# A bias that TensorE multiplied in is copied by ScalarE, and two convolution parts change place

## What is computed

```python
h = tok(x)                                    # conv, relu, batch norm: (16, 252, 256)
sim = q @ k.T * scale + bias[head, i - j]     # causal, 16 heads of 16
h = h + softmax(sim) @ v @ Wo + bo            # q, k, v from layernorm(h)
h = h + ffn_quantised(layernorm(h))           # 256 -> 768 -> 256
```

## Time and profile before

| | before |
|---|---|
| median of 3 runs | 801.44 us (800.09 to 801.98) |
| the profiled execution, own time | 804.09 us |
| its span, first to last instruction | 802.1 us |
| attention stage / feed-forward stage | to about 497 us / from there on |
| one step in the middle of the attention stage | 26.8 us |
| PE, DVE, ACT busy over the span | 78%, 76%, 57% |

### The profile page before, as it was taken

One profiled execution on the slowest core, in us unless ns is written; L12 is line 12 of the kernel. 1 busy time (PEld: TensorE's weight loads), 2 busy tenths in 40 slices (PEclk: granted clock), 3 DMA queues, 4 the chain that ended last, 5 costly groups with the idle time before them and its releaser, 6 DMA issues. The chain is left out here.

```text
span 802.1 us, 14667 instructions
## 1 busy us (share of the span) xinstructions
PE 625.1 (78%) x5169; PEld 463.1 (58%) x5169; DVE 610.3 (76%) x966; ACT 456.5 (57%) x647; POOL 134.7 (17%) x211
## 2 busy tenths in 40 slices
PE   4588899889988998899889975989999800005998
PEld 3457777767776777677767654335444300004997
DVE  7436787888788878888888787687479998994442
ACT  1436456545654565456545643426389966967772
POOL 4221122122213221322132000000024320000000
PEclk9789999999999999999999875899999955555999
DMA  7324313412441244124412311100134144400433
GB/s 199 114 30 48 40 21 61 62 26 33 59 59 25 34 59 59 23 36 59 61 25 30 55 54 53 39 1 0 44 150 194 44 188 145 138 0 1 145 118 100
DMA packets 39204, 52.82 MB, mean 66 GB/s; under 512 B 5724, under 2 KB 31772, under 8 KB 39164
## 3 DMA queue, kind: packets, MB, share of 16 engines
q1 hardware_dynamic: 38012, 51.49, 28.8%
q10 hardware_dynamic: 1152, 0.79, 0.5%
HBM read 22.74 MB, written 16.81 MB: 49 GB/s over the span
## 5 line engine op out<-in xcount | busy, mean ns | idle before, releaser
L803 DVE TENSOR_REDUCE mx<-ps 126x2 f32<-126x504 f32 (+1 forms) x192 | 125.7, 676 | 33.1 <-PE ps L651 31.8
L794 DVE TENSOR_TENSOR sbr<-ps,biasT 126x504 f32<-126x504 f32 x192 | 120.3, 676 | 27.6 <-PE ps L669 26.1
L879 ACT ACTIVATE pt<-sbr 126x504 f32<-126x504 f32 x192 | 110.9, 618 | 32.3 <-DVE sbr L794 26.1
L669 PE MATMUL ps<-q_st,k_st 66*126 66x252 f16 (+1 forms) x512 | 67.5, 257 | 22.7 <-DVE sbr L794 14.2
L648 PE MATMUL ps<-biasN,antib 126*126 126x504 bf16 x192 | 74.6, 388 | 3.6 <-DMA k_st<-kl 3.6
L651 PE MATMUL ps<-k_st,q_st 65*126 65x252 f16 (+1 forms) x512 | 74.0, 246 | 0.0
L1146 PE MATMUL ps<-x2t,wgT 128*128 128x504 f16 x288 | 67.2, 394 | 8.1 <-ACT gat L1437 4.7
L1423 PE MATMUL ps<-wdT,raws 128*126 128x256 f16 x480 | 67.5, 282 | 4.5 <-DVE raws L1364 4.5
L1122 PE MATMUL ps<-identf,sc 128*128 128x128 f32 x5 | 2.2, 435 | 86.7 <-DVE sc L1354 56.5
L651 PEld LDWEIGHTS ps<-k_st,q_st 65*126 65x126 f16 x512 | 59.6, 137 | 17.3 <-issue 2.5
L669 PEld LDWEIGHTS ps<-q_st,k_st 66*126 66x126 f16 x512 | 50.4, 142 | 32.9 <-DVE sbr L794 19.3
(11 more groups left out here) (189 smaller groups left out, 1405.4 us busy)
## 6 DMA issues: line engine op xcount, KB each, us to landing
up_raw<-raws SPq DMA_DIRECT2D x11, 756.0 KB, 3.2
x2t<-up_raw SPq DMA_DIRECT2D x6, 756.0 KB, 6.5
q_st<-qh SPq DMA_DIRECT2D x32, 128.0 KB, 3.7
k_st<-kh SPq DMA_DIRECT2D x32, 128.0 KB, 5.1
res<-hall SPq DMA_DIRECT2D x16, 252.0 KB
x2t<-res SPq DMA_DIRECT2D x16, 252.0 KB
out<-x2t SPq DMA_DIRECT2D x16, 252.0 KB
raws<-up_raw SPq DMA_DIRECT2D x5, 756.0 KB, 4.1
```

Source lines behind the costliest of these rows:

```text
L669: last = nc.tensor.matmul(ps[0:TT, score_bank[name, part], n * w:(n + 1) * w], kS[par][0:P2_ROWS, hd, kt], qS[par][0:P2_ROWS, hd, N - w:N] ...
L794: nc.vector.tensor_tensor(sbr[0:TT, n % 4].rearrange("p (h w) -> p h w", w=w), ps[0:TT, score_bank[name, n], 0:2 * N].rearrange("p (h w) - ...
L803: nc.vector.tensor_reduce(mx[0:TT, 0 if w == TT else 1, heads[0]:heads[-1] + 1], ps[0:TT, score_bank[name, n], 0:2 * N].rearrange("p (h w) ...
L879: nc.scalar.activation(pt[0:TT, n // 3 % 2, n % 3], sbr[0:TT, n % 4], ACT.Exp).then_inc(S["exp_r"], 1)
```

## The change

Of the 12 pieces of the first pass, pieces 3 to 11 no longer get their bias from a matmul. ACT copies it from `biasN` (bf16, in SBUF) into the PSUM bank (stage "seed"), and PE adds the scores to what lies there. Pieces 0 to 2 are as before, and the first sequence is wholly as before. Since ACT can't reverse rows, `biasN` must lie the right way round for the heads that are copied: in step 0, PE turns the six two-head pieces with the old matmul (`bias_product`) a piece ahead, and ACT copies each turned piece from its bank back into `biasN`. In the second pass only the first matmul of a piece carries `start`. In PE's order, parts 0 and 1 of the convolution stand ahead of the first piece of the second pass instead of after its fourth and fifth. In ACT's order the nine seeds are spread between `osb`, `va`, `xh`, `xn`, `onh` and `xnh`.

```diff
--- before.py
+++ after.py
@@ -100,7 +100,7 @@
             lines_dram bias_in flipT_ps biasT_r vec_ready rstd_ps cbx_r vec_in ident anti_in var_in pool_init dve_init act_init
             x_in xT_ps xh_r xl_r conv_ps relu_r v1_r h_r hb_r bns_r mv_r ve_r rstd_r nb_r xn_r
             xnT_ps xnh_r xnl_r q_ps k_ps v_ps qh_r ql_r kh_r kl_r va_r stack_in
-            p1_ps mx_r mT_ps mneg_r mneg_in p2_ps sb_r exp_r pv_ps osb_r oT_ps rc_r on_r onT_ps onh_r onl_r
+            seed_r flipN_ps p1_ps mx_r mT_ps mneg_r mneg_in p2_ps sb_r exp_r pv_ps osb_r oT_ps rc_r on_r onT_ps onh_r onl_r
             wo_ps h2_r spilled bns2_r mv2_r ve2_r rstd2_r nb2_r nm2_r nm_r xn2_r x2T_ps x2_r ax_r
             xi_r xqh_r xq_r ag_r ared par sc_r ap_r ao_r oq_r oh_r ol_r
             g_ps g_r u_ps raw_r au_r gq_r sig_r sq_r p_r g2_r uq_r o_r""".split()
@@ -446,8 +446,12 @@
             return [(kind, off, n) for n in range(first, end)]
 
         P2, P1 = pieces("P2", 0, 0, 12), pieces("P1", 1, 0, 12)
-        PE_ORDER = [("mT", 0, 0), ("q", 1, 0), ("q", 1, 1), ("k", 1, 0), ("k", 1, 1)] + P2[0:4] + [
-                    ("conv", 2, 0), P2[4], ("conv", 2, 1), ("x2T", -1, 0), P2[5], ("conv", 2, 2), P2[6], ("PV", 0, 0),
+        SEED = pieces("seed", 1, 0, 12)
+        FIRST_SEED = 3
+        SEEDS = 12 - FIRST_SEED
+        PE_ORDER = [("mT", 0, 0), ("q", 1, 0), ("q", 1, 1), ("k", 1, 0), ("k", 1, 1),
+                    ("conv", 2, 0), ("conv", 2, 1)] + P2[0:5] + [
+                    ("x2T", -1, 0), P2[5], ("conv", 2, 2), P2[6], ("PV", 0, 0),
                     ("conv", 2, 3), P2[7], ("conv", 2, 4), P2[8], ("conv", 2, 5), P2[9], ("PV", 0, 1), P2[10], P2[11],
                     ("v", 1, 0), P1[0], ("v", 1, 1), P1[1], ("PV", 0, 2), P1[2], P1[3], ("xT", 3, 0), P1[4],
                     ("PV", 0, 3), P1[5], P1[6], ("OT0", 0, 0), ("OT1", 0, 0), P1[7], P1[8], ("onT", 0, 0), P1[9],
@@ -457,7 +461,8 @@
                      ("onl", 0), P1[10], P1[11], ("xnl", 2)]
         ACT_ORDER = [("mneg", 0), ("qh", 1), ("kh", 1), ("xn2", -1)] + P2[0:3] + [("x2", -1)] + P2[3:7] + [
                      ("osb", 0, 0)] + P2[7:10] + [("relu", 2)] + P2[10:12] + [
-                     ("osb", 0, 1), ("va", 1), ("osb", 0, 2), ("xh", 3), ("osb", 0, 3), ("xn", 2), ("onh", 0),
+                     ("osb", 0, 1), SEED[3], ("va", 1), SEED[4], ("osb", 0, 2), SEED[5], ("xh", 3), SEED[6],
+                     ("osb", 0, 3), SEED[7], ("xn", 2), SEED[8], SEED[9], ("onh", 0), SEED[10], SEED[11],
                      ("xnh", 2)]
 
 
@@ -487,7 +492,7 @@
                 return order
             todo = []
             for st in order:
-                if runs(b, st[1]):
+                if runs(b, st[1]) and not (b == -1 and st[0] == "seed"):
                     todo += [st] + extra.get((b, st), [])
             return todo
 
@@ -548,6 +553,17 @@
                 last = nc.tensor.matmul(out_ap, a, w, start=(i == 0), stop=(i == len(todo) - 1))
             return last
 
+
+        TURNED = [n for n in range(FIRST_SEED, 12) if n % 3 < 2]
+
+        def turned_at(part):
+
+            return [n for i, n in enumerate(TURNED) if part == (FIRST_SEED - 1 if i == 0 else TURNED[i - 1])]
+
+        def bias_product(pe, part):
+            heads, w = piece_heads(part)
+            return nc.tensor.matmul(ps[0:TT, score_bank["P1", part], 0:2 * N], antib[0:TT],
+                                    biasN[0:TT, heads[0]:heads[-1] + 1, N - w:N], start=True, stop=True)
 
         def pe_step(pe, b, par):
             odd = 1 - par
@@ -641,12 +657,18 @@
                             wait(pe, "dve_init", INIT)
                             wait(pe, "biasN_in", 16)
                         wait(pe, "stack_in", 96 * (c + 1))
-                    score_free(pe, st, b)
+                    if part < FIRST_SEED or (isinstance(b, int) and b == -1):
+                        score_free(pe, st, b)
+                        bias_product(pe, part)
+                    if isinstance(b, int) and b == 0:
+                        for n in turned_at(part):
+                            score_free(pe, P1[n], b)
+                            bias_product(pe, n).then_inc(S["flipN_ps"], 1)
+                    if part >= FIRST_SEED and not (isinstance(b, int) and b == -1):
+                        wait(pe, "seed_r", SEEDS * (c - 1) + part - FIRST_SEED + 1)
                     heads, w = piece_heads(part)
                     qt = slice(0, TT) if w == TT else slice(TT, N)
                     dst = ps[0:TT, score_bank[name, part], 0:2 * N]
-                    nc.tensor.matmul(dst, antib[0:TT], biasN[0:TT, heads[0]:heads[-1] + 1, N - w:N],
-                                     start=True, stop=True)
                     for n, hd in enumerate(heads):
                         last = nc.tensor.matmul(dst[:, n * w:(n + 1) * w], qS[odd][0:P1_ROWS, hd, qt],
                                                 kS[odd][0:P1_ROWS, hd, 0:w], start=False, stop=True,
@@ -668,7 +690,7 @@
                     for n, hd in enumerate(heads):
                         last = nc.tensor.matmul(ps[0:TT, score_bank[name, part], n * w:(n + 1) * w],
                                                 kS[par][0:P2_ROWS, hd, kt], qS[par][0:P2_ROWS, hd, N - w:N],
-                                                start=True, stop=True)
+                                                start=(n == 0), stop=True, skip_group_check=True)
                     last.then_inc(S["p2_ps"], 1)
                 elif name == "PV":
                     g, vc = part, va[odd if off else par]
@@ -885,6 +907,19 @@
                     act.wait_ge(S["flipT_ps"], i + 1)
                     nc.scalar.activation(biasT[0:TT, 2 * i:2 * i + 2].rearrange("p h n -> p (h n)"),
                                          ps[0:TT, OB + i % 2, 0:2 * N], ACT.Copy).then_inc(S["biasT_r"], 1)
+                elif name == "seed":
+                    n = st[2]
+                    heads, w = piece_heads(n)
+                    bank = ps[0:TT, score_bank["P1", n], 0:2 * N].rearrange("p (h w) -> p h w", w=w)
+                    bias = biasN[0:TT, heads[0]:heads[-1] + 1, N - w:N]
+                    if isinstance(b, int) and b == 0 and n in TURNED:
+                        wait(act, "flipN_ps", TURNED.index(n) + 1)
+                        nc.scalar.activation(bias, bank, ACT.Copy).then_inc(S["seed_r"], 1)
+                    else:
+                        score_free(act, ("P1", off, n), b)
+                        if isinstance(b, int) and b < 2:
+                            wait(act, "seed_r", SEEDS * (c - 1) + n - FIRST_SEED)
+                        nc.scalar.activation(bank, bias, ACT.Copy).then_inc(S["seed_r"], 1)
                 elif name == "osb":
                     g = st[2]
                     wait(act, "pv_ps", 4 * c + g + 1)
```

## The result

| | before | after |
|---|---|---|
| median | 800.86 us (4 runs, 800.09 to 801.98) | 818.48 us (4 runs, 817.32 to 825.41) |
| ratio | 1 | 1.0237 (95% interval 1.0178 to 1.0295) |
| profiled execution, span | 802.1 us | 815.3 us |

The forecast was 814 us, range 795 to 827, slower with 0.59.

A forecast was written before the change was run, and what follows sets the result against it. PE was taken to set the pace from 259.33 to 270, DVE to 277.9, then a chain from onT. 14 x 1.1 us lost less 1.5 gained, 13.9 on the 801.44 median: 815.3, rounded down to 814; range 795 to 827.

The forecast's parts named there:

- The bound of each third of the step: PE sets the pace first, then DVE, then a chain into the next step; 1.95 us less PE work worth next to nothing.
- The convolution parts: Ahead of the second pass, hidden until DVE wants its first piece; 0.54 us off PE's path, 0.50 us carried on.
- The walk: Timeline of one step recomputed, all times 0.50 us early; wo 0.19 us earlier, held by seed 10.
- DVE's two waits that were to close: DVE's waits for PE of 0.75 and 0.68 us, up to 270.12 in the step; moving the convolution makes DVE 0.50 early.
- The copies: Nine ACT passes into PSUM at 0.59 us each, 5.3 us more ACT work a step, still under PE and DVE.
- The falls: PE's clock drops after the thin tail in three steps of four, 1.7 us each; 1.3 us a step, chance 0.52.
- Steps 1, 12 to 14 and the end: Steps 1 to 14 lose 1.1 us each; step 1 gains 1 us back and step 13 0.5.
- The clock holds: Rival: no falls in the loop, a gain of 0.19 us a step, 796 us (792 in a second form); chance 0.34.
- Seeds late: Rival: ACT's passes 0.2 us longer make seed 10 delay wo, without falls; 801.6 to 804 us, chance 0.10.

The follow-up runs named there:

- no_bias_matmul: The kernel before without the bias matmul of pieces 3 to 11 of the first pass in every step, and with no copies by ACT; 808.11 us.
- conv_first_only: The kernel before with only the two convolution parts moved ahead of the second pass; 796.87 us.
- fill_tail: The changed kernel with eight useless matmuls a step in the gaps of PE's tail; 798.47 us.
- seeds_first_six: The changed kernel with ACT's copies for pieces 0 to 5 alone, convolution parts still ahead of the second pass; 807.97 us.
- seeds_only: The changed kernel with the two convolution parts back in their old places; 831.32 us.

## Why the prediction was right, step by step

**The bound of each third of the step** held. The 1.95 us of PE work were worth 0.14 us a step where nothing else changed (no_bias_matmul, a step without a fall) and the same kind of work, taken from the stretch before, its full 0.64 us.

**The convolution parts.** They start 236.91 - 233.07 = 3.84 us into the step of the changed kernel, 3.83 forecast (257.12 - 253.29), released by `ql`. The wait ahead of the fifth piece shrank to 0.20 us. The gain was 0.27 and not 0.50 us (conv_first_only). The walk gave the first P2 piece 0.38 us from its start until DVE can read it, and it took 0.51 (238.02 to 238.53); and the wait of the first PV product grew by 0.12. Of DVE's two waits that were to close, the one of 0.75 us did (0.33), the one of 0.68 stayed as it was.

**The copies.** 592 ns each, 590 taken. The prediction names the Trainium skill's "ScalarE: Activation LUTs", which calls PSUM the lower-latency port for ScalarE's results (section "Step-by-step: what each stage is for"). This trace shows no gain against `onh`, 591 ns, which goes from PSUM to SBUF; its source and type differ too, so it is no clean test. The walk's waits are in the trace of a step without a fall, in their places and close in size: `xl` 1.25 (1.3), seed 8 0.73 (0.9), `on` 0.28 (0.5), seed 10 0.95 (1.3).

```profile
252.93 1.06 PE L719 MATMUL ps<-identf,osb 128*126 128x128 f32 x8 [1.25 <-DVE xl L831]
...
254.94 0.44 PE L673 MATMUL ps<-k_st,q_st 65*126 65x126 f16 x4 [0.73 <-ACT ps L922]
255.66 0.65 PE L727 MATMUL ps<-identf,on 126*128 126x126 f32 x4 [0.28 <-DVE on L866]
257.47 0.32 PE L673 MATMUL ps<-k_st,q_st 65*126 65x252 f16 x1 [0.95 <-ACT ps L922]
```

Piece 10 starts 24.40 us into the step, 24.33 forecast, and wo 25.33 against 25.20. A step gained 0.07 us without a fall, 0.19 forecast.

**The falls.** Forecast in three steps of four; eight of ten had them. The term that was mis-sized is their price: 1.3 us a step were forecast, from one low stretch of 3.4 us a fall at half its length. The low stretches were 3.4 to 10.2 us long, half of them 6.8, like the second one of the earlier trace rows and the one shown above, and the loss came to 28.65 - 26.73 = 1.9 us a step. The eight low stretches of steps 2 to 11 last 54.6 us together, 5.5 us a step, so the loss was a third of the low time and not half; part of it lies over PE's waits. Longer falls and a lower share partly cancelled.

**Steps 1, 12 to 14 and the end.** That the sum of the spans came out at 13.2 us against 13.9 forecast is in part luck, because the dearer falls met cheaper ends: step 1 gained 2.60 us against 1 forecast, steps 12 to 14 together lost 0.7 and not 3 x 1.1, and 3.3 us came off behind the last `mneg`. The end need not come from the change: over the twelve traces it takes between 331.0 and 335.4 us, 334.3 before and 331.0 after among them, in no order that follows the edits. Between the medians the loss was 17.6 us, with 12.6 forecast.

**The rivals.** "The clock holds" is ruled out for this kernel, and its price was about right: fill_tail, which holds the clock by force, is at 798.5 against 796. "Seeds late" is true as a mechanism (0.35 us a step, and 1.1 in seeds_first_six) and too small here. The rule of the Trainium skill cited in the prediction (page "TensorE: Matmul & The Clock Gate", section "A second HAM failure mode: psum-queue depth-cycling") says that PE's brief idles between groups, while it cycles through PSUM banks, can make the clock go up and down; the trace agrees, with a mean clock of 0.90 in steps 2 to 11. Two of the ten steps kept their clock, and the one from 233.79 to 260.52 had the same work and nearly the same waits in its tail, so a thin tail does not bring a fall each time. Which steps fall is not random either. The ten steps last 29.24, 29.14, 29.91, 28.23, 26.73 us and then nearly the same five again (29.25, 29.22, 29.90, 28.25, 26.64); in no_bias_matmul every third step has the fall, and in seeds_only every fourth is the one without. So something that repeats, but not with each step, decides as well. No run here shows what it is.

## What to carry to other kernels

Before moving work off an engine, read which engine sets the pace in that stretch of the step: the same copy was worth 0.21 us in one third of the step and nothing in the next. For TensorE look also at what is left behind, since a stretch in which it mostly waits, right ahead of a dense chain, can cost more than the work taken away saved; here it cost 2%. When the clock row of the page shows dips that repeat with the step, put work of no use into the gaps as a test: if the time falls, it is the clock, and the real cure is to take the work from somewhere else.

## What the runs showed of the hardware beyond that

- ScalarE writing 126x504 from bf16 in SBUF into PSUM took 592 ns, about as much as its copy out of PSUM (591 for `onh`), and 26 ns less than the exponential from SBUF to SBUF (618).
- A program made slower by leaving work out: nine bias matmuls a step less, 808.11 against 800.8 to 802.0 us, mean clock 0.95 against 1.00 in the same ten steps.
- The clock stayed low for 6.8 us after the fall at 283.55 although PE was busy 6.21 of 6.86 us in it.
